# First score tiles of an attention kernel fed straight from on-chip pieces, with the prologue reordered and two splits moved into the first sample

## What is computed

```python
emb = silu(_sin_emb(timestep)) @ W_ada + b_ada
scale, shift = split(emb[:, None, :], 2, axis=-1)
x = _ln(src) * (1.0 + scale) + shift
q, k, v = (x @ Wq + bq), (x @ Wk + bk), (x @ Wv + bv)      # 16 heads of 16
scores = einsum('bhqd,bhkd->bhqk', q / sqrt(16), k) + attention_bias
probs = softmax(where(src_mask, -inf, scores))
ctx = einsum('bhqk,bhkd->bhqd', probs, v)
x = x + (ctx @ Wo + bo)
h = _ln(x) * g2 + beta2
x = x + _gelu2(h @ W1 + b1) @ W2 + b2
x = adapter(rotate(adapter(x)))                            # each: down, gelu, expert, up, layer norm
```

## Time and profile before

| | us |
|---|---|
| median of 3 runs | 1001.78 (1001.27 to 1002.12) |
| the profiled execution | 1005.43, of which the span of the profile is 1003.6 |
| first score matmul | 41.56 after the span's start |
| DVE adds the bias of steps 0, 8, 12, 16, 17 | 42.42, 48.90, 53.21, 57.95, 64.27 |
| DVE adds the bias of step 24 | 75.7 |
| step 0 of the second sample on DVE | 125.5 |

### The profile page before, as it was taken

One profiled execution on the slowest core, in us unless ns is written; L12 is line 12 of the kernel. 1 busy time (PEld: TensorE's weight loads), 2 busy tenths in 40 slices (PEclk: granted clock), 3 DMA queues, 4 the chain that ended last, 5 costly groups with the idle time before them and its releaser, 6 DMA issues. The chain is left out here.

```text
span 1003.6 us, 20024 instructions
## 1 busy us (share of the span) xinstructions
PE 941.1 (94%) x5838; PEld 619.2 (62%) x5838; DVE 753.2 (75%) x2002; ACT 689.6 (69%) x1124; POOL 699.7 (70%) x540
## 2 busy tenths in 40 slices
PE   5879999999998999999999899989999999999996
PEld 4646656655655665665565566555477777777573
DVE  7787878789869787887878888788444765668466
ACT  3377888798788789778879787978644444444332
POOL 2468788788869778877876987876554545557465
PEclk9889999999999999999999999999999999999998
DMA  8977996996897799599689879966111110111101
GB/s 271 300 294 265 371 359 229 342 389 239 297 389 284 278 361 357 196 335 384 237 292 372 333 242 342 372 250 232 64 64 43 42 43 22 42 64 42 43 22 63
DMA packets 127533, 229.96 MB, mean 229 GB/s; under 512 B 6512, under 2 KB 53872, under 8 KB 123632
## 3 DMA queue, kind: packets, MB, share of 16 engines
q1 hardware_dynamic: 127472, 229.26, 63.0%
HBM read 187.30 MB, written 41.94 MB: 228 GB/s over the span
## 5 line engine op out<-in xcount | busy, mean ns | idle before, releaser
L935 ACT ACTIVATE prob<-prob,nmax 128x512 f32<-128x512 f32 x512 | 356.9, 729 | 60.5 <-DVE nmax L760 57.7
L760 DVE CUSTOM_DVE_ANT_0 prob<-s_bank,big 128x512 f32<-128x512 f32 x512 | 339.4, 686 | 70.1 <-POOL big L1099 31.2
L1099 POOL TENSOR_TENSOR big<-big,mterm_early 128x2048 f32<-128x2048 f32 (+2 forms) x88 | 305.2, 3484 | 72.4 <-DMA big<-in_fside_Bx16xSxS 63.0
L591 PEld LDWEIGHTS t_bank<-ident,prob 128*128 128x128 f32 x2048 | 239.8, 141 | 167.9 <-issue 53.5
L591 PE MATMUL t_bank<-ident,prob 128*128 128x128 f32 x2048 | 318.4, 278 | 15.6 <-ACT prob L935 6.7
L942 ACT COPY pt<-t_bank 128x512 f32<-128x512 f32 x312 | 181.4, 584 | 58.0 <-PE t_bank L591 56.4
L579 PE MATMUL s_bank<-stack_k,stack_q 128*128 128x512 bf16 x512 | 196.5, 384 | 1.9 <-DVE nmax L760 1.6
L769 DVE COPY pt<-t_bank 128x512 f32<-128x512 f32 x200 | 137.5, 688 | 40.9 <-PE t_bank L591 40.6
L605 PE MATMUL o_bank<-pt,val 128*32 128x512 f32 x1024 | 122.9, 598 | 1.2 <-ACT pt L942 0.7
L2173 POOL TENSOR_TENSOR gl<-big,gh 128x512 fp32r<-128x512 f32 x64 | 83.1, 1306 | 49.4 <-DVE gh L1723 49.4
L2032 ACT ACTIVATE big<-bank,late 128x512 f32<-128x512 f32 x62 | 42.7, 690 | 72.6 <-PE bank L1438 69.0
(11 more groups left out here) (245 smaller groups left out, 1464.9 us busy)
## 6 DMA issues: line engine op xcount, KB each, us to landing
big<-in_fside_Bx16xSxS SPq DMA_DIRECT2D x128, 1024.0 KB, 8.0
pieces_dram<-pieces SPq DMA_DIRECT2D x64, 384.0 KB, 7.2
stack_q<-pieces_dram SPq DMA_DIRECT2D x15, 1024.0 KB, 8.1
stack_k<-pieces_dram SPq DMA_DIRECT2D x15, 1024.0 KB, 9.4
pieces_dram<-pieces SPq DMA_DIRECT2D x32, 256.0 KB, 7.4
xin<-in_x SPq DMA_DIRECT2D x8, 512.0 KB, 8.8
x_dram<-x SPq DMA_DIRECT2D x8, 512.0 KB, 2.6
x1r<-x_dram SPq DMA_DIRECT2D x8, 512.0 KB, 4.4
```

What stands on the lines that cost most here:

```text
L591: last = pe.transpose(t_bank[n % 2][:, c * P:(c + 1) * P], prob[:, n % NT, c * P:(c + 1) * P], ident[:])
L760: dve.tensor_tensor_reduce(out=prob[:, n % NT, :], in0=s_bank[n % 3][:, :], in1=bias[:, h % NB, t, :], scale=-1.0, scalar=3e38, op0=ALU.ad ...
L935: act.activation(tile, tile, ACT.Exp, bias=nmax[:, n % NT:n % NT + 1], scale=-1.0).then_inc(exped.sem, 1)
L1099: pool.tensor_tensor(bias[:, h % NB, tiles], bias[:, h % NB, tiles], mterm[:, tiles], ALU.add).then_inc(masked.sem, 1)
```

## The change

Five edits go together.

1. The first head's stacks no longer go through DRAM: 16 small DMAs, each 16 partitions x 512 bfloat16 (16 KB), copy from `pieces` to `stack_q` and `stack_k` inside SBUF. The 8 for Q are issued on SP, ahead of each store of that piece; the 8 for K on ACT's queue, ahead of its projection u = 2. Step 0 waits for all 16 (`first_head_in`); step 4 waits for heads 1 and 2, which now are the first stack load. `keep_busy` at the end of the prologue shrinks from 25 + 25 matmuls with a wait between them to 8.
2. Cuts 2 and 3 leave the prologue. DVE makes them inside the first sample, at n = 5 and n = 9; their pieces are stored at head 3 and loaded at heads 4 and 5.
3. `domains` moves to n = 13 of the first sample, `rotations` behind the low part of wk; the low part of wk comes after `xtl`, that of wv after cut 1.
4. In PE's prologue each of Q, K and V waits only for its own weights.
5. POOL adds the mask to head 1's bias only after cut 1, no longer right after `xtl`.

```diff
-FIRST_HEADS = 2
+FIRST_HEADS = 3
+FIRST_STORE_1_AT, FIRST_STACK_1_AT, FIRST_CUTS_AT, DOMAINS_AT = 3, (4, 5), (5, 9), 13
...
+        def load_first_head(eng, qk, product):
+            eng.dma_start((stack_q, stack_k)[qk][product * HD:(product + 1) * HD, 0],
+                          pieces[0:P:HC, qk, PRODUCTS[product][qk]]).then_inc(first_head_in, 16)
...
                     sp.wait_ge(piece_made, 3 * qk + i + 1)
+                    if qk == 0:
+                        for product in range(3 * i, 3 * i + n):
+                            load_first_head(sp, 0, product)
...
-                    if h in STACK_1_AT:
-                        load_stack(b - 1, 1, STACK_1_AT.index(h), first=first)
+                    if first and h == FIRST_STORE_1_AT:
+                        store_pieces(-1, 1, first=True)
+                    if h in (FIRST_STACK_1_AT if first else STACK_1_AT):
+                        load_stack(b - 1, 1, (FIRST_STACK_1_AT if first else STACK_1_AT).index(h), first=first)
...
-            for heads, arrived in ((slice(0, FIRST_HEADS), first_heads_in), (slice(FIRST_HEADS, HC), stack_in[0].sem)):
+            for heads, arrived in ((slice(1, FIRST_HEADS), first_heads_in), (slice(FIRST_HEADS, HC), stack_in[0].sem)):
...
-            store_pieces(-1, 1, first=True)
...
                 if first and n == 0:
+                    pe.wait_ge(first_head_in, 2 * NP8 * 16)
+                elif first and n == QT:
                     pe.wait_ge(first_heads_in, 2 * 16)
...
-                if use[0] in "QV":
-                    ready = 2 if use[0] == "Q" else 3
+                if use[0] in "QKV":
+                    ready = " QKV".index(use[0])
...
-            keep_busy(pe, o_bank, wh["wq"][:, 0], 25)
-            pe.wait_ge(pieces_out[0][1].sem, pieces_out[0][1].at(-1, 48))
-            keep_busy(pe, o_bank, wh["wq"][:, 0], 25)
+            keep_busy(pe, o_bank, wh["wq"][:, 0], 8)
...
+                    if first and n in FIRST_CUTS_AT:
+                        cut(2 + FIRST_CUTS_AT.index(n))
+                    if first and n == DOMAINS_AT:
+                        setup["domains"](dve)
...
-            dve.wait_ge(weights_in, 16 * len(later))
-            dve.wait_ge(w_high, 3)
-            dve.tensor_tensor(wl["wv"], w["wv"], wh["wv"], ALU.subtract).then_inc(w_low, 1)
+            low_weight("wk", 2)
+            dve.tensor_copy(ident_bf[:], k["ident"][:]).then_inc(ident_bf_made, 1)
+            setup["rotations"](dve)
             cut(0)
             cut(1)
+            dve.wait_ge(weights_in, 16 * len(later))
+            low_weight("wv", 3)
             spare_use(banks, at["V", 0], -1, first=True)
-            cut(2)
             spare_use(banks, at["V", 1], -1, first=True)
-            cut(3)
...
+                    if first and u == 2:
+                        for i_piece in range(3):
+                            act.wait_ge(piece_made, 3 + i_piece + 1)
+                            for product in range(i_piece, NP8, 3):
+                                load_first_head(act, 1, product)
...
-            pool.wait_ge(xtl_done.sem, xtl_done.at(-1, DC))
+            pool.wait_ge(cut_done.sem, cut_done.at(-1, 2))
```

More of the change, by code:

```diff
@@ L375, in attention_block @@
         piece_made, first_heads_in = sem("piece_made"), sem("first_heads_in")
+        first_head_in = sem("first_head_in")
         w = dict(wq=con[:, 0:2], wk=con[:, 2:4], wv=x1[:, 0].rearrange("p (c n) -> p c n", c=DC),
@@ L843, in spare_use @@
                                              ALU.add, ALU.add).then_inc(x1_done.sem, 1)
[L845 to L857, removed]
-                    if last and n == NORMALISE_LAST:
-                        normalise(b, banks)
-                    for m, use in enumerate(banks.uses):
-                        if use[2] + parts(use[0]) == n and not (first and use in TAIL):
-                            spare_use(banks, m, b)
-                    if n == (LOW_LAST if last else LOW_STEP):
-                        low_parts(b)
-                if last:
-                    for m in range(len(LAST), len(banks.uses)):
-                        spare_use(banks, m, b)
             def cut(u):
@@ L872, in cut @@
                 if u >= 2:
+                    dve.wait_ge(first_head_in, 2 * NP8 * 16)
                     dve.wait_ge(pieces_out[0][u % 2].sem, pieces_out[0][u % 2].at(-1, 48))
@@ L890, in cut, with iteration @@
                     dve.wait_ge(cut_done.sem, cut_done.at(-1, u + 1))
+            def iteration(b, first=False, last=False):
+                banks = SpareBanks("last" if last else "middle")
+                for n in range(STEPS + 1):
+                    if n + 2 < STEPS:
+                        add_bias(b, n + 2)
+                    elif n < STEPS and not last:
+                        add_bias(b + 1, n + 2 - STEPS)
+                    if n - 1 in DVE_TAKES:
+                        take_turned(b, n - 1)
+                    if first and n in FIRST_CUTS_AT:
+                        cut(2 + FIRST_CUTS_AT.index(n))
+                    if first and n == DOMAINS_AT:
+                        setup["domains"](dve)
+                    if not last and n == STATISTICS_AT:
+                        statistics(b)
+                    if not last and n == NORMALISE_AT:
+                        normalise(b)
+                    if last and n == NORMALISE_LAST:
+                        normalise(b, banks)
+                    for m, use in enumerate(banks.uses):
+                        if use[2] + parts(use[0]) == n and not (first and use in TAIL):
+                            spare_use(banks, m, b)
+                    if n == (LOW_LAST if last else LOW_STEP):
+                        low_parts(b)
+                if last:
+                    for m in range(len(LAST), len(banks.uses)):
+                        spare_use(banks, m, b)
             dve.memset(eps[:], EPS).then_inc(consts, 1)
@@ L897, in _ @@
             statistics(-1)
-            setup["domains"](dve)
-            setup["rotations"](dve)
             normalise(-1)
@@ L903, in _, with low_weight @@
             dve.wait_ge(early_in, 16 * len(early))
-            for m, name in enumerate(("wq", "wk")):
-                dve.wait_ge(w_high, m + 1)
+            def low_weight(name, made):
+                dve.wait_ge(w_high, made)
                 dve.tensor_tensor(wl[name], w[name], wh[name], ALU.subtract).then_inc(w_low, 1)
+            low_weight("wq", 1)
             dve.tensor_scalar(bq_scaled[:], vec["bq"], HD ** -0.5, None, ALU.mult).then_inc(bq_made, 1)
-            dve.tensor_copy(ident_bf[:], k["ident"][:]).then_inc(ident_bf_made, 1)
             at = {use[:2]: m for m, use in enumerate(banks.uses)}
```

## The result

The changed kernel takes 1011.69 us (median of 6, 1007.20 to 1014.28) where the kernel before takes 1001.52 (median of 6, 999.29 to 1004.06): a ratio of 1.0105, 95% interval 1.0088 to 1.0121 (a ratio here is estimated from all executions; the quotient of these two medians is 1.0102, and for e11 below it is 1.0005 where the ratio is 1.0017). It is slower by 1%, where the forecast had 0.63%; sign and range held. One execution of the kernel before, in the session of e9 to e12, took 1170.12 us at a granted clock of 0.76 and is left out of every ratio.

What follows compares the result with a forecast made beforehand. TensorE bounds the kernel from step 24 to the second sample, so the change was priced by step 24's start: -4.1 + 11.5 - 0.1 - 0.6 + 2.4 + 1.4 - 4.2 = +6.3 on 1001.8, giving 1008.1 us, range 1000.0 to 1012.5.

Steps and rivals of the forecast that it cites:

- Start, -4.1: Prologue: first score matmul earlier than 41.56 by 4.1 us, taken between -5.1 (DVE first) and -3.1 (POOL first).
- The tie: End of cut 1 releases both wv's low part on DVE and POOL's 4.1 us mask; which goes first was left open.
- Cut 2, +11.5: Cut 2 at step 7: its four instructions wait for POOL's masks of heads 3, 4, 5 and a late term, 11.5 us.
- its own test, under 5 us: Stated check in the changed kernel's profile: the forecast is wrong if cut 2 takes under 5 us.
- landing time of 5.5 us: Head 4's bias lands 5.5 us after being asked for, 0.5 to 0.8 us before head 3's mask ends.
- POOL blocks once: Rival: POOL blocks only cut 2's first instruction, 4.5 us; cut 3 meets head 5's mask, +1.7; 1001 to 1004; chance 0.13.
- Cut 3, +2.4: Cut 3 after step 11: head 6's bias comes late, POOL has nothing to add, so the cut takes 2.35 us.
- Steps 12 to 17, +1.4 - 4.2: First sample: `domains` adds 1.4 us; the normalisation meets no mask and takes 1.4 for 5.58, 4.2 less.
- the +1.7: Steps 12 to 17: `domains` may wait for head 6's mask, 0 to +1.7 us; set at zero with steps 17 to 24.
- Second stacks, 0: Step 32: the second stacks may come up to 1 us late; left at zero.
- The first head isn't early: Rival: small copies or stacks of heads 1 and 2 arrive late, first scores start as before; +10.4, 1012; chance 0.09.
- Faster: Rival: start gain whole and cuts between POOL's masks, -6.6 or -3.8 us, 995 to 998; chance 0.16.

Runs made afterwards that it cites:

- e11: Changed kernel with e1's order, e3's stacks, e5's holds, small copies behind projection u = 2, and head 6's mask onward held for the next x's low part: ratio 1.0017.
- e9: Changed kernel with cuts 2 and 3 back in the prologue and masks from head 6 on held until the next sample's low part of x: ratio 1.0014.
- e12: Kernel before with edit 5 alone, plus masks from head 6 on held until the next sample's low part of x is made: ratio 0.9986.
- e1: Changed kernel with the low part of wv made ahead of cut 0 instead of behind cut 1: ratio 1.0101 to the kernel before.
- e3: Changed kernel with the second half's pieces stored at head 2 and their stacks loaded at heads 3 and 4, one head earlier: ratio 1.0088.
- e6: Kernel before with edit 2 alone: cuts 2 and 3 at n = 5 and 9, stores and stacks at heads 3, 4 and 5: ratio 1.0071.
- e7: Kernel before with head 1's mask behind cut 3, the copy of x ahead of it, and the last filler cut from 25 to 8: ratio 0.9978.
- e5: Changed kernel with POOL's masks of heads 3 and 4 held behind cuts 2 and 3, head 5's behind the normalisation: ratio 1.0052.
- e10: e7 plus masks from head 6 on held until the low part of the next sample's x is made: ratio 0.9968 to the kernel before.

## Why the prediction was right, and where its sizes were off

**Start, -4.1.** Right in size: -3.7. The tie went to POOL, and the first score matmul came at 38.4, the figure given for that case. Two terms were off and made up for each other. Q started 2.0 us earlier and not 0.7, because the filler ahead of it moved as well (it ends at 18.94, for 20.04). And ACT's eight issues took 5.34 us where the upper bound was 3.2, so its projection came 1.6 us later than in before and not 0.6; e1 shows that V waits for it until 30.56 even when DVE wins.

**Cut 2, +11.5.** The mechanism was right and the sum of its four prices close: 10.3 in e1 (1.84, 0.69, 3.19, 4.48 against 2.5, 3.65, 4.35, 1.05) and 10.2 in e3. One of the four slipped between two masks, and the last took the mask that I had laid on the one before. In the profiled execution of after it took 3.94 us, and by its own test, under 5 us, that would be the forecast wrong. The term hung on a landing time of 5.5 us with half a microsecond of margin, which the rival "POOL blocks once" names. The bias landed after 7.0. Here the sum was wrong by most, 7.6 us (+3.8 from step 0 to 8 for +11.4), and the step that failed is that landing time. It was taken from another stretch (69 to 86) of before; head 4's own load, issued at 45.05, took 7.6 us to land there, and head 5's, at 48.87, 9.0. In e1 it took 5.5.

**Cut 3, +2.4.** This step failed where cut 2 slips through. I had put 1.7 us for head 5's mask into that rival; it cost 4.0 more (6.38 for 2.35), since the late mask terms queue behind that mask, and the last three instructions of the cut took turns with them. So the total of both cuts depends little on which is hit: 10.3 in after, 12.6 in e1 and e3. The profiled execution of after is that rival, "POOL blocks once" (3.94 us for its 4.5), to which I had given 0.13. Its 1001 to 1004 was too low by cut 3 and by the second stacks.

**Steps 12 to 17, +1.4 - 4.2.** -3.2 in after for -2.8. In e1 and e3 it was -1.7 and -0.6, as `domains` waited for head 6's mask, the +1.7 that I had set at zero together with steps 17 to 24.

**Second stacks, 0.** Wrong in after by +3.2; I had allowed them "up to 1 us". The K stack took 10.1 us to land. e3 removes the wait, and what that is worth stays open, as its ratio can't be told from after's.

**Sum.** +6.3 was forecast; +6.0 stands at the second sample in the profiled execution of after. That agreement is luck: cut 2 came 7.6 us below its term, and cut 3 and the second stacks 7.2 us above theirs. Between the medians it is +10.2. In e1 and e3, where cut 2 is blocked as forecast, it is +8.7, and their medians are 1% above before as well. That the slower executions of after are of e1's kind is argued from this and not shown: there is only the trace of its fastest. Of the 10.2 us between the medians some 1.5 stay open. One candidate is my base. The profiled execution of before was 3.9 us above its median. It had 2.5 us of low clock ahead of step 0 (e6) and a blocked normalisation (5.58 us); where another execution has neither, the start gain of 4.1 and the relief of 4.2 are credited too high. The table speaks for it: the starts of the second sample, measured against the profile of before, make nearly every kernel look better than its ratio (e7: -6.5 us against -2.2). So does the quickest execution of before, 995.49 us: less the 875.5 that follows the second sample in the quickest profiles, it leaves an estimated 120 us for the start of that sample, and not 125.5. But what follows varies by 6 us, and one profile of each kernel doesn't settle it.

**What the masks don't explain.** In the forecast 9 us of cut 2 were POOL's blocking, and the small copies and the new order were a gain of 4.1 at the start. Holding POOL back returned 5.3 of the 10.5 us (e5). With hardly any blocking left, e11 still loses 4.0 us against e10, and the small copies, the new order and the late second stacks without the moved cuts 2.8 (e9 against e12).

**The rivals.** "The first head isn't early" fell: the last small copy had landed by 32.1, and step 0 did not wait for it. "Faster" fell: none of the six executions of after is below 1007.

**The rule.** DVE was blocked for whole instructions in every run here but e10, by 3.9 us at L921 after a tie of 0.01. The Trainium skill (SBUF — State Buffer, "Who interferes with whom") states that an instruction of DVE with two SBUF inputs contends with GpSimd, and one with a single SBUF input outside the two-port modes doesn't; the trace agrees: L921 was blocked, and `add_bias`, with its other operand in PSUM, took 0.69 us at 49.54 beside the mask of 48.43.

## What to carry to other kernels

Before moving work of VectorE that reads two SBUF operands or casts, lay it beside GpSimd's list at the new place, and price each instruction of the chain at one whole GpSimd instruction, since GpSimd gets in between two of them. If it has to stand there, make GpSimd wait for it: three waits returned 5 us here. Where a collision depends on a landing time with a margin of half a microsecond, price both outcomes to the end of the next collision, because a chain that slips past one mask meets the next. When an engine that computes also issues DMAs, look at who waits for its next result: here eight issues on ScalarE held up V, and TensorE's clock fell while it waited.

## What the hardware showed that I had not expected

ACT's issue of a small copy (16 KB, 16 partitions, within SBUF) cost more than the 0.33 to 0.37 us of the two issues in the earlier trace rows; I had taken 0.4. Eight take 5.34 us, 0.67 each, and hold up ACT's own list meanwhile; the first three of SP's take 0.62 each. It need not be the small copy that is dear: SP's six stores of pieces took 0.36 each in before and 0.48 to 0.83 in after, where both queues issue in the same stretch. Which of the two it is stays open.

```profile
24.40 5.34 ACTq L419 DMA_DIRECT2D stack_k<-pieces  x8
29.79 0.69 ACT L1000 ACTIVATE proj<-spare,bq_scaled 128x512 f32<-128x512 f32 x1 [7.22 <-issue]
```

```profile
21.79 1.86 SPq L419 DMA_DIRECT2D stack_q<-pieces  x3
```

They land soon, in the median 2.2 to 2.3 us after their issue (DMA issues of the stretch 21 to 30: count, KB each, us to landing):

```profile
stack_q<-pieces SPq DMA_DIRECT2D x8, 16.0 KB, 2.2
stack_k<-pieces ACTq DMA_DIRECT2D x8, 16.0 KB, 2.3
```

The blocking works in both directions: head 4's mask took 3.53 us in e1, where the mean of that shape is 3.12, and the four late mask terms took 3.45 in after beside cut 3, against 2.71 in e10.
